# The last slot's rows of a mixture-of-experts sum, written on their own after the copy of the sums

## What is computed

```python
def _L1_ffn_ref(x, gate_kernel, w0_kernel, w1_kernel, wo_kernel):
    gate_logits = jnp.einsum('bsd,de->bse', x, gate_kernel)
    top_k_weights, top_k_indices = jax.lax.top_k(gate_logits, TOP_K)
    top_k_weights = jax.nn.softmax(top_k_weights, axis=-1)
    one_hot = jax.nn.one_hot(top_k_indices, NUM_EXPERTS)
    combine = jnp.einsum('bsk,bske->bse', top_k_weights, one_hot)
    h0 = jnp.einsum('bsd,edm->bsem', x, w0_kernel)
    h1 = jnp.einsum('bsd,edm->bsem', x, w1_kernel)
    inter = jax.nn.silu(h0) * h1
    return jnp.einsum('bse,bsem,emd->bsd', combine, inter, wo_kernel)
...
x = x + jnp.tanh(g_xattn[1]) * _L1_xattn_ref(_layernorm(x), ctx_512, ctx_512, ...)
x = x + jnp.tanh(g_ffn[1]) * _L1_ffn_ref(_layernorm(x), ...)
return x
```

## Time and profile before

| | us |
|---|---|
| median of 3 runs | 1776.29 (1775.36 to 1776.71) |
| the profiled execution | 1775.91 |
| its span, first to last instruction | 1774.0 |
| last add issued by POOL, from the span's start | 1753.31 |
| first DMA of the copy issued by SP | 1758.10 |
| last DMA of the copy landed | 1773.6 |
| TensorE busy | 1459.5 (82% of the span) |
| mean granted TensorE clock | 0.902 of full speed |

### The profile page before, as it was taken

One profiled execution on the slowest core, in us unless ns is written; L12 is line 12 of the kernel. 1 busy time (PEld: TensorE's weight loads), 2 busy tenths in 40 slices (PEclk: granted clock), 3 DMA queues, 4 the chain that ended last, 5 costly groups with the idle time before them and its releaser, 6 DMA issues. The chain is left out here.

```text
span 1774.0 us, 30923 instructions
## 1 busy us (share of the span) xinstructions
PE 1459.5 (82%) x10394; PEld 771.0 (43%) x10395; DVE 1030.4 (58%) x1689; ACT 1016.8 (57%) x1551; POOL 767.9 (43%) x717
## 2 busy tenths in 40 slices
PE   6666666686999869999997207999999999999994
PEld 2444544462444424444443103444444444444442
DVE  3899999797999778888864723060550502360000
ACT  4999999934666547777774403444444444444441
POOL 3000000015667528888884354354444544453342
PEclk9678777788999969999997658999999999999997
DMA  9411100000000000000002464151643422431113
GB/s 336 160 30 43 48 25 1 31 1 1 1 1 1 1 1 3 3 3 3 3 3 89 165 265 153 31 159 43 177 120 81 133 68 62 139 106 27 32 25 107
DMA packets 49259, 118.86 MB, mean 67 GB/s; under 512 B 5536, under 2 KB 5792, under 8 KB 48576
## 3 DMA queue, kind: packets, MB, share of 16 engines
q1 hardware_dynamic: 34832, 88.53, 14.5%
q0 software_dynamic: 8176, 18.65, 5.4%
q10 hardware_dynamic: 6144, 10.28, 2.0%
HBM read 84.21 MB, written 37.43 MB: 69 GB/s over the span
## 5 line engine op out<-in xcount | busy, mean ns | idle before, releaser
L1633 PE MATMUL PS<-R 128*128 (+1 forms) x1872 | 432.9, 381 | 9.1 <-issue 7.9
L429 ACT ACTIVATE R<-R 128x512 bf16<-128x512 f32 x448 | 278.9, 709 | 10.8 <-PE PS L449 5.0
L1787 DVE TENSOR_SCALAR R<-wring 128x1024 f16<-128x1024 f32 x56 | 60.3, 1088 | 384.0 <-PE PS L1656 350.9
L1633 PEld LDWEIGHTS PS<-R 128*128 128x128 f16 x1872 | 179.3, 98 | 218.3 <-issue 20.2
L449 PE MATMUL PS<-R,ident_b 128*128 128x256 bf16 (+1 forms) x1056 | 171.8, 325 | 85.1 <-ACT R L429 81.2
L1823 POOL TENSOR_TENSOR R<-R 128x512 f32<-128x512 f32 x78 | 114.5, 1468 | 293.4 <-ACT R L1731 182.2
L1656 PE MATMUL PS<-R 128*128 (+1 forms) x936 | 214.8, 379 | 1.2 <-ACT R L1743 1.2
L1047 DVE TENSOR_REDUCE R<-PS 128x1 f32<-128x512 f32 x256 | 166.6, 685 | 45.5 <-PE PS L1229 42.9
L1025 POOL TENSOR_TENSOR R<-R 128x512 f32<-128x512 f32 x128 | 166.6, 1301 | 28.5 <-ACT R L1152 12.7
L1152 ACT ACTIVATE R<-PS 128x512 f32<-128x512 f32 x256 | 144.4, 598 | 41.3 <-PE PS L1243 40.8
L449 PEld LDWEIGHTS PS<-R,ident_b 128*128 128x128 bf16 x1056 | 116.2, 122 | 118.0 <-ACT R L429 91.5
(11 more groups left out here) (267 smaller groups left out, 2478.0 us busy)
## 6 DMA issues: line engine op xcount, KB each, us to landing
wring<-in_L_ffn_w_kernel_dram SPq DMA_DIRECT2D x48, 512.0 KB
slot_rows<-R SPq DMA_DIRECT2D x1, 10023.0 KB, 40.4
R<-slot_rows ACTq DMA_DIRECT2D x39, 257.0 KB, 2.7
R<-in_L_ffn_w_kernel_dram SPq DMA_DIRECT2D x16, 512.0 KB, 5.9
wring<-in_L_ffn_wo_kernel_dram SPq DMA_DIRECT2D x16, 512.0 KB
R<-in_L_ffn_wo_kernel_dram SPq DMA_DIRECT2D x16, 512.0 KB, 4.6
X<-in_x_dram SPq DMA_DIRECT2D x4, 1024.0 KB, 9.1
R<-in_L_ffn_w_up_dram SPq DMA_DIRECT2D x4, 1024.0 KB, 10.2
```

The costliest lines, as they stand in the source:

```text
L429: nc.scalar.activation(marks[:, j * S:(j + 1) * S], SIM[:, tile * S:(tile + 1) * S], ACT.Sign, bias=cfloat[:, tile:tile + 1], scale=-1.0). ...
L1633: mm = nc.tensor.matmul(bank[2 * half + g], ZT[n][:, (4 * pz + k) * P:(4 * pz + k + 1) * P], weights(place, at), start=(i % 12 == 0), stop ...
```

## The change

SP no longer waits for all 39 adds but for the first 38, and then copies `ACC` to `out` as before. POOL waits until the copy has landed (`stored`), and only then adds the last slot into `ACC`. After that POOL waits for its own add and issues two more indirect DMAs of 128 rows of 2 KB: one gathers the last slot's rows from `ACC` into `last_rows` (part of R3 in SBUF, where `SL[0]` was), the other writes them to their places in `out`. The row numbers of both, `LIDX`, are the last slot's, masked with 2047 by one DVE instruction, so that padding rows fall on tokens 0 to 127 and rewrite what these hold. SP ends on the second DMA's semaphore, `last_out`.

```diff
+        lidx_set = sem("lidx_set"); last_in = sem("last_in"); last_out = sem("last_out")
+        LIDX = R1[:, 14480:14481].bitcast(I32)
+        last_rows = R3[:, 0:512]
@@ dve_experts, at its end
+            v.wait_ge(tagged, NSLOT * 2 + 2)
+            nc.vector.tensor_scalar(LIDX, SIDX[:, NSLOT - 1:NSLOT], NT * P - 1, None,
+                                    ALU.bitwise_and).then_inc(lidx_set, 1)
@@ pool_slots
+            def finish():
+                pool.wait_ge(added, NSLOT * 16)
+                pool.wait_ge(lidx_set, 1)
+                pool.wait_ge(it32, NSLOT * 2)
+                nc.gpsimd.indirect_dma_start(
+                    out=last_rows, out_offset=None, in_=ACC[0:NT * P, :],
+                    in_offset=bass.IndirectOffsetOnAxis(ap=LIDX, axis=0)).then_inc(last_in, 16)
+                pool.wait_ge(last_in, 16)
+                nc.gpsimd.indirect_dma_start(
+                    out=out.rearrange("b s d -> (b s) d"), out_offset=bass.IndirectOffsetOnAxis(ap=LIDX, axis=0),
+                    in_=last_rows, in_offset=None).then_inc(last_out, 16)
...
+            pool.wait_ge(stored, NB * 16)
             add(NSLOT - 1)
+            finish()
@@ sync
-            sp.wait_ge(added, NSLOT * 16)
+            sp.wait_ge(added, (NSLOT - 1) * 16)
             for b in range(NB):
                 sp.dma_start(out[b], ACC[b * S:(b + 1) * S, :]).then_inc(stored, 16)
-            sp.wait_ge(stored, NB * 16)
+            sp.wait_ge(last_out, 16)
```

## The result

| | before | after |
|---|---|---|
| median | 1776.71 us (15 runs, 1772.6 to 1778.45) | 1779.11 us (15 runs, 1777.65 to 1780.77) |
| ratio to before | 1 | 1.0016, 95% interval 1.0009 to 1.0023 |
| a second measurement on another occasion | 1776.28 us (21 runs) | 1778.44 us (11 runs), ratio 1.0010, interval 1.0001 to 1.0019 |
| span of the profiled execution | 1774.0 us | 1775.8 us |

The change costs 0.16%, where I had forecast 0.07% less. 1779.11 lies outside the range (1772.7 to 1778.7). It is within 0.2% of the time before, which the forecast took for the least that can be told; with 15 runs on each side the interval is narrower than that (0.07% to either side of the ratio), and both measurements have it above 1. The second one was expected at 1.0010 to 1.0023.

The account below looks back on a forecast made before the run. The end was taken as a serial chain, its 15.5 us copy with no engine computing beside it. Copy start -13.9 us, then +12.7 us for add, gather, write and releases: -1.2 us, median 1775.1 us, range 1772.7 to 1778.7.

Parts of the forecast that it names:

- The start of the copy: SP's copy waits for slot 37's add instead of the last: from 1758.1 to 1744.2, 13.9 us earlier.
- The length of the copy: Same four DMAs beside working engines: 15.5 us as before, bounds 13.9 and 16.5; last landing 1759.7.
- The wait on POOL and the add: Slot 38's add waits for the copy, starts at 1760.0, 6.7 us later than before, and lands 4.8 us later, 1764.8.
- The gather: POOL's indirect read behind the add: 0.3 us release plus 3.5 us, bounds 2.8 and 4.8; landing 1768.6.
- The write: POOL's indirect write to out behind the gather: 0.3 us release plus 3.5 us, bounds 3.2 and 4.8; landing 1772.4.
- The end: From the last write's landing to the end of the span: 0.4 us, giving 1772.8.
- the copy hidden in full: Rival: copy lands before 1753.0, so POOL does not wait; needs under 8.8 us; median 1768.4; chance 0.03.
- long indirect DMAs: Rival: gather and write cost 6.6 us each, like the scatter's first pass; median 1781.3; chance 0.05.
- slow instruction loading: Rival: an instruction load waits behind the copy, 8.8 us for median 1777.2, or 15.5 us for 1783.9; chance 0.05.
- Short transfers: Rival: gather and write at ACT's 2.8 us each; median 1773.7, or 1772.1 with a 13.9 us copy; chance 0.07.

Follow-up runs that it names:

- before_wait: Kernel before, plus a wait for the copy's landing at the end of POOL's stream: span 1783.1 us, tail 40.2 us against 34.4.
- sum_on_chip: Changed kernel, last slot's rows gathered beside the copy, summed by VectorE on chip, one write behind the copy: 1772.64 us, ratio 0.9975 to before.
- two_slots: Like sum_on_chip, but the copy starts after slot 36's add and slots 37 and 38 are both patched into out: 1768.86 us, ratio 0.9954 to before.
- three_drains: two_slots with slot 37's write moved behind slot 38's compute, plus two more POOL drains where it stands idle: 1760.79 us, ratio 0.9907 to before.

## Why the prediction was wrong

By its own steps, with the changed kernel's profile (whose slot 37 is 0.17 us later than before):

- **The start of the copy**, 1744.2: 1744.39. Right.
- **The length of the copy**, 15.5 us beside a busy core: 15.2. Right. The engines didn't slow it down, and TensorE's last matmuls took 2.76 us as before.
- **The wait on POOL and the add**, 1760.0 and 4.8 us: 1759.83, and the next DMA 4.94 us later. Right.
- **The gather**, 3.5 us: 3.5. Right, and for the right reason: its issue took 1.03 us, like the scatter's 0.96 to 1.24, and not like the add's 1.58.
- **The write**, 3.5 us: 2.7, under the lower bound of 3.2 that I had from the scatter, whose last DMA had others ahead of it. That was 0.8 us in the kernel's favour. The price that I had quoted from the Trainium skill ("DMA: Bandwidth & Descriptors", section "Anatomy of one DMA — SWDGE (gpsimd) path"), 2.6 us, fits this one and is 0.9 us short for the gather.
- **The end**, 0.4 us from the last landing to the end of the span: 4.6. This is the step that failed. I took the 0.4 us from the kernel before, where SP's wait for the copy is the last thing to end, and carried it over to a kernel in which POOL ends last. An engine's end has its own price, and POOL's, 5.9 to 6.2 us in this kernel, lay in the trace of before, hidden under the copy, with 12.5 us to spare.

In sum: the last landing came 1.2 us earlier than forecast and the end 4.2 us later behind it, 3.0 us on a span of 1772.8, which is the 1775.8 measured. In the tail this is +1.6 us against before, 0.09%, at the lower end of the first interval and inside the second. The medians show +2.4 and +2.2 us; what the further 0.6 to 0.8 us are, no profile shows. Of the 4.0 us between the forecast's 1775.1 and 1779.11 another 0.4 are the time before itself, 1776.71 with 15 runs where three had given 1776.29.

The rivals: the copy hidden in full, long indirect DMAs and slow instruction loading did not occur (one packet of instructions was loaded beside the copy, between 1754 and 1756; the last matmuls, over by then, had run on time). Short transfers did in part (the write). The case that came true, slower by a mechanism of its own, was on no list. I had asked of every instruction put behind the copy what it costs, and not what it had cost the engine to be finished 20 us early: the change made POOL the last engine to end, and that alone had a price.

What stays open: whether the drain counts DMAs or their rows (each of these has 128), whether plain DMAs of POOL count as well (here it issues none), why a gather beside the copy waits for it, and why TensorE ran its last matmuls at the lower clock in some profiles and not in others.

## What to carry to other kernels

Before a change moves the last work of a kernel from one engine to another, read how long each engine takes to end, in the rows of the program's last line; the longest of them is hidden as long as another engine is last by more than that. On GpSimd, after many indirect DMAs, clear the backlog with a drain at a place where it waits anyway: one such line turned this change from 0.16% slower into 0.16% faster. And don't count on hiding a small DMA beside a large copy once the copy has been issued: here it landed with it. Whether it would land in time if issued just ahead of the copy, I have not run.

## What the runs showed that I had not expected

- A drain of GpSimd grows with the indirect DMAs issued since the last one, long after they have landed: 2.8 us for 32, 3.1 for 37, 5.9 for 70, 5.9 for 71 (before_wait), 6.0 for 73, and 0.04 us when nothing was issued in between.
- An indirect DMA of 128 rows of 2 KB, issued beside a DRAM-to-DRAM copy of 4 MB, took 12.1, 12.2 and 12.3 us to land in three kernels instead of 3.2 to 3.6, though it was on another queue; none of its packets moved in the first 5 us (sum_on_chip, two_slots). In three_drains it was issued 7.2 us after the copy's start instead of 3.4 to 3.6 us, and took 8.6 us. In all four it landed 15.7 to 15.8 us after the copy's start. The Trainium skill ("DMA: Bandwidth & Descriptors", section "Queues, rings and completion order") has the DMA engines go round robin between queues packet by packet; one packet of instructions did get through in mid-copy here, but the gather saw little of such turns.
- The write of the last slot's rows took 2.7 us without and 2.1 to 2.2 us with the check for padding rows; how many rows that skipped, I have not counted.
